# Four attention layers on one core: softmax units of the small layers cut by token half, sums of squares on ScalarE, and a new order of steps

## What is computed

```python
xn = rmsnorm(x, norm_w)                       # x * rsqrt(mean(x*x) + eps) * w
q = (xn @ wq)                                 # 16 heads of 8
k, v = cond @ wk, cond @ wv                   # 4 key/value heads of 8, each used by 4 query heads
attn = softmax(q k^T / sqrt(8))               # over the 64 context tokens
x = x + (attn v) @ wo
```

## Time and profile before

| | |
|---|---|
| median of the runs | 1511.9 us |
| the profiled execution | 1509.35 us |
| its span, first to last instruction | 1507.5 us |
| busy in the span | PE 97%, weight loads 77%, DVE 71%, ACT 73%, POOL 51% |
| TensorE's granted clock, mean | 0.990 of full |
| DMA | 36.92 MB, mean 24 GB/s |
| chain that ended last | PE 93%, DVE 2%, issue, SP's queue, ACT and POOL 1% each |

### The profile page before, as it was taken

The page is one execution under the profiler, slowest core; times in us unless marked ns, Lnnn a source line. Parts: engine busy times, 40 slices in busy tenths (PEclk is TensorE's granted clock), DMA queues, the critical chain, the costliest instruction groups (busy, mean ns, idle before and its releaser), DMA issues.

```text
span 1507.5 us, 56267 instructions
## 1 busy us (share of the span) xinstructions
PE 1462.3 (97%) x23872; PEld 1167.3 (77%) x23872; DVE 1072.9 (71%) x2291; ACT 1107.7 (73%) x2529; POOL 773.0 (51%) x881
## 2 busy tenths in 40 slices
PE   7999999999999999999999999999999999999875
PEld 5787878887878877877887877877777787878763
DVE  1467777777777777777777777777777777777875
ACT  3577777787777777777787777777777787777764
POOL 3345555445555445555445555445555455555643
PEclk9999999999999999999999999999999999999987
DMA  5100000100000100000001001110000100000000
GB/s 153 28 21 14 24 21 24 26 20 21 25 24 22 26 22 19 25 24 21 26 16 25 25 21 25 25 27 15 24 22 23 26 16 17 18 14 18 17 11 8
DMA packets 57178, 36.92 MB, mean 24 GB/s; under 512 B 16864, under 2 KB 55776, under 8 KB 56928
## 3 DMA queue, kind: packets, MB, share of 16 engines
q1 hardware_dynamic: 56032, 33.22, 8.6%
q10 hardware_dynamic: 896, 0.10, 0.0%
HBM read 16.49 MB, written 4.19 MB: 14 GB/s over the span
## 4 chain that ended last, share of the span: by engine, by line
PE 93%; DVE 2%; issue 1%; SPq 1%; ACT 1%; POOL 1%; DMA 0%; POOLq 0%; ACTq 0%
PE bank L398 15%; PE bank L457 15%; PE bank L390 15%; PE bank L475 8%; PE bank L425 7%; PE bank L448 6%; PE bank L494 6%; PE bank L437 4%; PE bank L466 4%; PE bank L357 3%; PE bank L500 3%; PE bank L481 3%; PE bank L413 2%; PE bank L406 2%; DVE st L657 1%
## 5 line engine op out<-in xcount | busy, mean ns | idle before, releaser
L341 POOL TENSOR_TENSOR E<-E,st 128x512 f32<-128x512 f32 x512 | 533.3, 1042 | 667.4 <-DVE st L668 667.4
L665 DVE TENSOR_REDUCE st<-E 128x8 f32<-128x512 f32 x512 | 341.1, 666 | 194.7 <-ACT E L573 143.9
L573 ACT ACTIVATE E<-E,inv 128x256 f32<-128x256 f32 x768 | 347.9, 507 | 14.9 <-DVE E L661 7.6
L578 ACT COPY E<-bank 128x512 f32<-128x512 f32 x512 | 286.4, 587 | 58.3 <-PE bank L457 57.7
L457 PE MATMUL bank<-ident,E 128*128 128x128 f32 x2048 | 289.1, 277 | 11.5 <-POOL E L341 11.4
L657 DVE TENSOR_REDUCE st<-bank 128x8 f32<-128x512 f32 x384 | 251.6, 677 | 64.2 <-PE bank L448 60.6
L457 PEld LDWEIGHTS bank<-ident,E 128*128 128x128 f32 x2048 | 243.7, 143 | 49.8 <-POOL E L341 14.6
L661 DVE TENSOR_TENSOR E<-bank,st 128x512 f32<-128x512 f32 x384 | 256.1, 674 | 0.0
L390 PE MATMUL bank<-cT,wk 128*128 128x256 f32 x1024 | 247.5, 385 | 2.7 <-ACT cT L522 2.3
L398 PE MATMUL bank<-wv,cT 128*128 128x512 f32 x512 | 247.0, 605 | 0.0
L390 PEld LDWEIGHTS bank<-cT,wk 128*128 128x128 f32 x1024 | 186.5, 192 | 27.5 <-ACT cT L522 2.7
(11 more groups left out here) (62 smaller groups left out, 1701.8 us busy)
## 6 DMA issues: line engine op xcount, KB each, us to landing
KB<-K SPq DMA_DIRECT2D x1536, 8.0 KB
cin<-in_ctx SPq DMA_DIRECT2D x32, 256.0 KB, 3.7
xin<-in_x SPq DMA_DIRECT2D x32, 128.0 KB, 2.6
out<-xN SPq DMA_DIRECT2D x32, 128.0 KB, 2.0
wk<-in_L_xattn_Wk SPq DMA_DIRECT2D x2, 512.0 KB, 8.0
wv<-in_L_xattn_Wv SPq DMA_DIRECT2D x2, 512.0 KB, 9.8
wq<-in_L_xattn_Wq SPq DMA_DIRECT2D x1, 512.0 KB, 9.2
wo<-in_L_xattn_Wo SPq DMA_DIRECT2D x1, 512.0 KB, 5.3
```

The lines of the kernel that those rows point to most:

```text
L341: e.tensor_tensor(E3, E3, wide(stat[s][u][:, 16:24]), ALU.mult).then_inc(g_nrm.sem, 1)
L573: m = e.activation(E[s][u][:, 256 * p:256 * p + 256], E[s][u][:, 256 * p:256 * p + 256], ACT.Exp, scale=inv[s][:, p:p + 1])
L578: e.copy(E[s][u][:, :], bank_of["t", g, l, u][:, :]).then_inc(a_et.sem, 1)
L665: e.tensor_reduce(stat[s][u][:, 8:16], heads(E[s][u][:, :]), AX, ALU.add).then_inc(d_sum.sem, 1)
```

## The change

A unit u of a small layer becomes a token half p = u // 2 with two of the four head sets, those in two neighbouring score banks (r = u % 2). The scores matmuls write where they did, but the four score banks are one tensor `scores` [128, 4, 512], so that a unit's maximum and subtraction read 256 columns in each of two banks. All rows of a unit now have one scale, and its exponential is one call of 512 columns. pv takes its moving operand from the unit and columns where it now lies. ssq on VectorE goes: x2 is two Square calls of 128 columns, each with its sum in ScalarE's accumulator output. All five tables are new. The period is 44.84 in place of 44.96. The order on TensorE is now, with the bursts in brackets: q0 [pv3 s1] wo3; k [pv2] v; wo2 [s0.0 s0.1] xt; cT [s3 pv1] k; t0 [pv0.0 pv0.1 s2] k. At the start k.0, v.2 and v.3 stand ahead of the third group's cT, and k3 of group 0 comes three steps (v.3, v.1 and the next group's k.1) later. In SP's order a group's three kr now stand at 113.17, 132.27 and 140.29, and xT at 168.5.

```diff
-PERIOD = 44.96
+PERIOD = 44.84
...
-    "s": {0: (140.31, 144.76), 1: (176.38,), 2: (207.52,), 3: (241.24,)},
+    "s": {0: (130.94, 132.25), 1: (162.91,), 2: (195.62,), 3: (224.99,)},
...
-    "pv0": {0: (161.41, 163.5)},
-    "wo0": {0: (167.5,)},
+    "pv0": {0: (147.15, 147.83)},
+    "wo0": {0: (154.44,)},
...
-    "kr": {1: (118.77,), 2: (174.8,), 3: (152.3,)},
-    "xT": {0: (208.33,)},
-    "st": {0: (275.86,)},
+    "kr": {1: (113.17,), 2: (132.27,), 3: (140.29,)},
+    "xT": {0: (168.5,)},
+    "st": {0: (279.65,)},
...
-        banks = [ctx.enter_context(nc.psum_tensor(f"bank{i}", [128, 512], F32)) for i in range(8)]
+        scores = ctx.enter_context(nc.psum_tensor("scores", [128, 4, 512], F32))
+        banks = [ctx.enter_context(nc.psum_tensor(f"bank{i}", [128, 512], F32)) for i in range(4)]
...
+        def pairs(ap):
+            return ap.rearrange("p (r h k) -> p r h k", r=2, k=64)
...
-                held[i] = ("add" if l == 0 else "sub", g, l, unit)
-                bank_of["scores", g, l, unit] = banks[i]
+                if l == 0:
+                    held[i] = ("add", g, l, unit)
+                    scores_of[g, l, unit] = scores[:, i, :]
+            for unit in units if l else ():
+                p, r = unit // 2, unit % 2
+                held[at[2 * r + p]] = ("sub", g, l, unit)
+                scores_of[g, l, unit] = scores[:, at[2 * r]:at[2 * r] + 2, 256 * p:256 * p + 256].rearrange(
+                    "p r (h k) -> p r h k", k=64)
+            bank_of[st] = at
...
                 elif kind == "ms":
-                    w.wait_ge(d_ssq, ("ssq", g, l, 0))
+                    w.wait_ge(a_x2, ("x2", g, l, 0))
...
-                                n, c = 256 * (b // 2) + 128 * gp + 64 * (b % 2), 96 * (l - 1) + 32 * gp
+                                n, c = 256 * (r % 2) + 128 * gp + 64 * (b % 2), 96 * (l - 1) + 32 * gp
                                 m = e.matmul(bank[32 * r:32 * r + 32, 64 * b:64 * b + 64], VBg[:, b, c:c + 32],
-                                             E[s][r][:, n:n + 64], start=(gp == 0), stop=(gp == 1))
+                                             E[s][2 * (b // 2) + r // 2][:, n:n + 64], start=(gp == 0), stop=(gp == 1))
...
-                        for p in range(NP):
-                            m = e.activation(E[s][u][:, 256 * p:256 * p + 256], E[s][u][:, 256 * p:256 * p + 256],
-                                             ACT.Exp, scale=inv[s][:, p:p + 1])
-                        m.then_inc(a_exp.sem, 1)
+                        e.activation(E[s][u][:, :], E[s][u][:, :], ACT.Exp, scale=inv[s][:, u // 2:u // 2 + 1]
+                                     ).then_inc(a_exp.sem, 1)
...
-                    else:
-                        w.wait_ge(d_ssq, ("ssq", g, l - 1, 0))
-                    e.activation(QT[s][:, 2, :], xN[s][:, :, :].rearrange("p k c -> p (k c)"), ACT.Square
-                                 ).then_inc(a_x2.sem, 1)
+                    if g >= NS and l == 1:
+                        w.wait_ge(g_inv, ("ms", g - NS, 3, 0))
+                    elif l > 1:
+                        w.wait_ge(g_inv, ("ms", g, l - 1, 0))
+                    for p in range(NP):
+                        m = e.activation(QT[s][:, 2, C * p:C * p + C], xN[s][:, p, :], ACT.Square,
+                                         accum_out=nt[s][:, 0, p:p + 1])
+                    m.then_inc(a_x2.sem, 1)
...
-                    e.tensor_reduce(stat[s][u][:, 0:8], heads(bank_of["scores", g, l, u][:, :]), AX, ALU.max
+                    e.tensor_reduce(stat[s][u][:, 0:8].rearrange("p (r h) -> p r h", r=2), scores_of[g, l, u], AX, ALU.max
                                     ).then_inc(d_max.sem, 1)
                 elif kind == "sub":
                     w.wait_ge(d_max, ("max", g, l, u))
-                    e.tensor_tensor(heads(E[s][u][:, :]), heads(bank_of["scores", g, l, u][:, :]),
-                                    wide(stat[s][u][:, 0:8]), ALU.subtract).then_inc(d_sub.sem, 1)
+                    e.tensor_tensor(pairs(E[s][u][:, :]), scores_of[g, l, u],
+                                    stat[s][u][:, 0:8].rearrange("p (r h a) -> p r h a", r=2, a=1).to_broadcast(
+                                        [128, 2, 4, 64]), ALU.subtract).then_inc(d_sub.sem, 1)
...
-                elif kind == "ssq":
...
```

More of the change, by code:

```diff
@@ L70 @@
[L70 to L74, removed]
+    "cT": {0: (2.11,)},
+    "k": {0: (81.64, 53.64, 64.06, 94.88)},
+    "v": {0: (70.95, 97.41, 85.83, 86.11)},
+    "k3": {0: (100.56,)},
+    "v3": {0: (112.64,)},
+    "xT": {0: (97.22,)},
+    "q0": {0: (120.99, 119.07, 119.88, 123.66)},
+    "exp": {0: (135.6, 139.11, 140.42, 136.56),
+            1: (170.71, 169.68, 166.18, 169.92),
+            2: (200.83, 206.57, 197.63, 204.22),
+            3: (237.77, 238.77, 240.93, 231.82)},
@@ L75 @@
+    "et": {0: (142.27, 144.46, 146.34, 146.69),
+           1: (179.58, 177.31, 176.11, 179.67),
+           2: (210.29, 213.74, 210.7, 213.96),
+           3: (248.61, 248.34, 244.86, 243.78)},
+    "pv0": {0: (149.88, 150.03)},
+    "x2": {1: (162.29,), 2: (196.95,), 3: (220.49,)},
+    "xt": {1: (157.94,), 2: (187.87,), 3: (218.85,)},
+    "q": {1: (160.97,), 2: (190.79,), 3: (224.08,)},
+    "pv": {1: (181.9,), 2: (215.23,), 3: (253.08,)},
 }
 DVE_TIME = {
-    "add": {0: (141.49, 143.93, 149.28, 146.82)},
@@ L78 @@
[L78 to L95, removed]
+    "add": {0: (130.07, 135.75, 135.05, 131.62)},
+    "max": {0: (131.07, 136.18, 136.09, 135.41),
+            1: (165.39, 164.87, 163.38, 169.59),
+            2: (198.75, 198.05, 195.51, 197.48),
+            3: (227.58, 227.06, 237.56, 225.97)},
@@ new lines @@
+    "sum": {0: (136.99, 139.14, 141.76, 143.83),
+            1: (173.4, 171.58, 169.83, 171.64),
+            2: (201.59, 207.2, 203.32, 206.7),
+            3: (239.04, 239.53, 242.34, 238)},
+    "rcp": {0: (138.73, 140.79, 141.97, 145.68),
+            1: (174.07, 172.05, 171.43, 174.98),
+            2: (205.08, 207.47, 206.38, 207.34),
+            3: (243.75, 241.14, 243.29, 238.77)},
+    "wo0": {0: (155.44,)},
+    "sub": {1: (169.79, 168.62, 167.19, 171.36),
+            2: (199.51, 201.24, 198.56, 200.37),
+            3: (237.59, 236.37, 238.36, 229.04)},
@@ L227, in xattn_kernel @@
             before[st] = [held[i] for i in at if held[i]]
-            bank_of[st] = [banks[4 + i] for i in at] if st[0] == "pv0" else banks[4 + at[0]]
+            bank_of[st] = [banks[i] for i in at] if st[0] == "pv0" else banks[at[0]]
             for i in at:
@@ L428, in tensor_program @@
                 elif kind == "s" and l == 0:
-                    bank = [bank_of["scores", g, 0, 2 * u + h2] for h2 in range(2)]
                     w.wait_ge(a_ev, *[("q0", g, 0, i) for i in range(4)])
@@ L447, in tensor_program @@
                                 lo, b = 32 * r, 2 * p + b2
-                                m = e.matmul(bank_of["scores", g, l, r][64 * b2:64 * b2 + 64, 256 * p:256 * p + 256],
+                                m = e.matmul(scores[64 * b2:64 * b2 + 64, bank[r], 256 * p:256 * p + 256],
                                              QT[s][lo:lo + 32, 0, 64 * b:64 * b + 64],
```

75 lines of the change are left out of this document (26 added, 49 removed).

## The result

The changed kernel takes 1525.18 us (median of six executions), the kernel before 1512.04 in the same runs: a ratio of 1.0083, 95% interval [1.0066, 1.0100]. It is 0.8% slower, and outside the range. One of the six took 2116.57 us at a mean granted clock of 0.652 (the others have 0.985 to 0.989) and is not in the ratio; the median of the other five is 1523.53. The profiled execution took 1522.73 us, its span is 13.4 us longer than before's.

What follows compares the result with a forecast made beforehand. TensorE's pace was taken to bound the middle, VectorE's work and hops the tail of some 100 us. From 1509.35 us, -6.0 - 2.8 - 1.7 - 1.5 = -12.0 gave 1497.35, 1499.9 as a median; range 1491.0 to 1508.0.

Steps and rivals of the forecast that it cites:

- The joins: TensorE, s0.1 behind s0.0 and pv0.1 behind pv0.0: each join saves 0.11 us, 59 of them 6.5 us.
- wo3 behind s1: TensorE, a full step behind small ones in place of two transposes: 0.02 us more per group, 0.6 in all.
- The stalls: TensorE's "issue" stops in the pv0 burst, read as late instructions: half of 5.5 us goes, -2.8, bounds -5.5 and +5.5.
- rival B: Joined steps, the densest 256 instructions, stall 0.75 us in every group: slower, 1520.5 us; chance 0.07.
- s3, 1.8 us to spare: Score banks, the tightest turn found: the last add ends some 5.0 us after s0.0 starts, s3 comes at 6.8.
- The start: First groups: waits of k3 (0.99 us) and s1 (0.51) go, t0.0 is 0.3 late; -1.7, bounds -2.5 and +1.
- ScalarE, VectorE: Exponential 0.63 to 0.75 us, x2 0.6, max and subtract unchanged, all covered by TensorE in the middle; busy near 1030 and 1035.
- The tail: Last groups and last layer: fewer VectorE sums, shorter exponential waits, a later second reciprocal; -1.5 us, bounds -4 and +1.5.
- the 0.4 that I had worked out: Last layer, VectorE: two sums instead of one ahead of the second reciprocal, +0.4 us.
- The 1.4 us that fewer sums were to save in the tail: Tail, VectorE: seven sums of 0.39 us, 2.8 in all, fall away, about half of it on the path, -1.4.

Runs made afterwards that it cites:

- e5: The changed kernel, but SP issues the context load and the store between the second and third key load, away from the pv0 burst: 1523.56 us, ratio 1.0087.
- e4: The changed kernel, but ScalarE copies v3 out of its bank ahead of the exponential exp2.0 (one slot): 1519.80 us, ratio 1.0057.
- e7: The changed kernel with k.2 between pv0.1 and s2, v3 ahead of wo0, and its copy ahead of et3.2 on ScalarE: 1542.58 us, ratio 1.0204.
- e13: The changed kernel with v3 and xt1 behind all three t3 on TensorE and behind their copies on ScalarE, pv0 still joined: 1516.98 us, ratio 1.0038.
- e10: The changed kernel with s2 between the two pv0, v3 right behind wo0 and its copy one et earlier on ScalarE: 1522.42 us, ratio 1.0068.
- e11: The changed kernel with v3 right behind wo0 and its copy one et earlier on ScalarE, pv0 still joined: 1523.65 us, ratio 1.0080.
- e1: The changed code with the old order of steps (tables of the kernel before, less ssq): 1512.09 us, ratio 1.0007 against the kernel before.
- e2: The code of the kernel before with the new order of steps (new tables, ssq put back): 1542.78 us, ratio 1.0199 against the kernel before.

## Why the prediction was wrong

**The joins: right in kind, undersized.** 0.11 was forecast, 0.16 each measured, -0.32 a group, -9.4 over the 59 joins for the -6.5 written. The one pair of the old trace takes 2.14, those in mid-stream now 2.09; and the rows gave 1.10 - 0.98 = 0.12 in any case. wo3 behind s1 costs 0.10 where I took 0.02, less 0.06 of the two t2 that I had counted the wrong way round: near 0.04 net.

**The stalls: the step that failed by its sign.** Taken at -2.8 "because the load moves away", measured +7.2, outside my own bound of +5.5. The place was read rightly, and so was "instructions that arrive late"; what makes them late was not: one window with 139 GB/s beside one stall was made a cause, and e5 shows stalls at 10 GB/s. I even looked only at the x load; the context load, of twice its size, moves into the burst. What counts in its place is how fast 256 instructions follow each other: 2.4 to 2.8 us in the new burst, 2.8 to 2.9 in the old one. The rival B had the mechanism, the joined steps as the densest 256 instructions. It had it at 0.07, in every group at 0.75 us each, with a break-even at 20 groups; measured are 10 long periods of 26 with 1.4 us each (before: 9 with 0.75). Only 10, since the place moves against the group, which has 746 matmuls: numbered from 0, the matmuls 9800, 10556, 11312 and 12069 come late, one group and ten matmuls apart, until the place has left the burst, and the next is 18750, nine groups on. The queue of instruction transfers stood on the page of before. What sets the moment at which such a transfer starts isn't shown.

**The bank wait at v.0: the step that was missing.** I checked the score banks (s3, 1.8 us to spare, and in the middle of the kernel it never waits) and the turns of data, and not the four other banks, which turn with every step. +0.46 a group, 31 x 0.46 = 14 us, the largest term of the result. e4, e7 and e13 each take part of it away, 0.22, 0.27 and 0.29 on the beat; the other 0.17 are read from rows. It outweighs the joins. Without it and with my stall term the sum would have come out near the forecast.

**The start: right.** k3 no longer waits, s1 of the first group starts without a gap; the first wo0 is 2.3 earlier (-1.7 forecast, bounds -2.5 and +1). TensorE's timeline after:
```profile
25.96 1.03 PE L424 MATMUL bank<-cT,wks 128*96 128x256 f32 x4
...
63.53 1.12 PE L458 MATMUL scores<-KB,QT 32*64 32x256 f32 x32
```
The number is less sure than it looks: e10's first wo0 is at 58.96 and e11's at 55.93, though they differ by s2's slot alone.

**ScalarE, VectorE: right in their steps.** Their busy times, 1057.7 and 1055.9, stay above the 1030 and 1035 written. The exponential takes 736 ns (0.63 to 0.75 forecast), maxima 679, unchanged. x2 now is two calls and two reads of the accumulator, an instruction that I did not expect:
```profile
408.54 0.34 ACT L601 ACTIVATE QT<-xN 128x128 f32<-128x128 f32 x1
408.74 0.23 ACT L601 ACTIVATION_READ_ACCUMULATOR QT<-xN 128x1 f32 x1
408.83 0.34 ACT L601 ACTIVATE QT<-xN 128x128 f32<-128x128 f32 x1
409.03 0.23 ACT L601 ACTIVATION_READ_ACCUMULATOR QT<-xN 128x1 f32 x1
```
From 408.54 to 409.26 it is 0.72, inside 0.45 to 0.83. e1 confirms that all of this is covered in the middle.

**The tail: wrong by sign.** -1.5 forecast, bounds -4 and +1.5; +1.1 measured behind the last wo0. The tail that I priced reaches further back, and the last two periods take 80.6 us for 78.4, +2.3, so from the wo0 two groups ahead of the last it is +3.3, outside the bounds. One execution of each is thin evidence for that: e1's ten executions spread over 6.4 us. In the last layer VectorE's first maxima come 18.6 us ahead of the end, 16.7 before. The chain up to GpSimd's last product is longer by the 0.4 that I had worked out (10.08 for 9.70 us), as the rows show; before is the earlier trace rows.
```profile
1502.32 1.89 DVE L668 TENSOR_REDUCE st<-scores 128x8 f32<-128x512 f32 x3 [4.27 <-PE scores L458]
...
1507.98 1.04 POOL L352 TENSOR_TENSOR E<-E,st 128x512 f32<-128x512 f32 x1 [7.40 <-DVE st L680]
1509.36 3.04 POOL L352 TENSOR_TENSOR E<-E,st 128x512 f32<-128x512 f32 x3 [0.34 <-DVE st L680]
```
The other 1.5 lie behind it. TensorE, hardly busy for the 9 us ahead, is there at its lower clock level (1.2 GHz, 0.50), and in the last stretch it comes back to 2.4 GHz for less of the time: a mean of 0.64, where the last 10.5 us before had 0.77. That this clock is the whole of the 1.5 isn't shown. The window after:
```profile
1509.00:1520.90 11.90, 6.51 (x84) 5.38 (x84) 1.50 (x6) 2.71 (x5) 3.06 (x4) 0.64 0.04 12
```
The 1.4 us that fewer sums were to save in the tail appear nowhere; where they went is open.

**The sum, again,** an estimate with each term of the group taken 31 times: start -2.3, joins 31 x -0.32 = -9.9, wait at v.0 +14.3, wo3, t2 and q0 steps +2.5, stalls +7.2, end +1.1: +12.9 of the 13.4.

## What to carry to other kernels

In an order written out by hand, each step's cover belongs to the ring of buffers as well as to the data: for every short step, sum TensorE's time from the filling of its buffer to the next use of the same buffer, and set against it what the copying engine does in that time. A new order of a full engine should be judged in parts (code alone, order alone, one slot at a time), since here a gain of 0.3 us a group and a loss of 0.5 hide in one number. Where an engine stops for "issue", number its instructions and see whether the stops keep their place in the stream while their times move, and look for the landings of the "instruction" queue: here the stops came where 256 instructions of TensorE would pass in less than 3 us, and a less dense step between the two dense ones, s2, all but halved the loss. And a transfer that runs beside a stall is no cause until a kernel without it has lost the stall.

## What the runs showed of the hardware

- Two steps of small matmuls of one tile shape, joined, save 0.16 us: 2.03 us for 128 of 64x64, against 1.09 to 1.10 for each 64 alone.
- TensorE stops for "issue" within bursts of small matmuls at some 8 ns for each load or matmul, for up to 1.9 us, with 5% of the DMA engines busy and full clock. All 138 such stops stand at the same place of a block of 256 of its instructions, and end 1.1 to 1.6 us behind the landing of a transfer of 16384 bytes in the "instruction" queue, of which there are 189 for 189 x 256 instructions. Over the periods 3 to 28 this cost 7 to 8.5 us with 160 matmuls in a burst and s2 between the pv0, 14 to 15 with the pv0 joined (9.4 in e2, where waits for copies take up part), 26 with a further burst of 192.
- A Square of 128x128 with its sum accumulated is two instructions on ScalarE, 319 and 209 ns; two such pairs took 0.72 us; an exponential of 128x512 with its scale from memory is 736 ns, where two of 256 columns took 0.91.
